# Where a preLN decoder layer's self-attention stage takes its inverse square roots: ACT's roots and DVE's reciprocals, or a power on POOL

## The chip, the cores and the metric

One core of one Trainium2 chip runs the whole kernel in one launch. The core has five engines with a queue each: PE (matrix products and transposes), DVE (vector work), ACT (scalar functions, copies with scale and bias), POOL (the general-purpose vector cores, called GpSimd) and SP (only DMA issues here). An engine works through its own instructions in program order and waits on semaphores that others raise. The metric is device time in microseconds (us), the median over runs, lower is better.

## The reference

Input `x` is 32 sequences of 128 tokens of 128 features, float32. One decoder layer is three residual blocks. Only the first (and the layer norm of the second) is touched here:

```python
def _layernorm(x, axis=-1, eps=1e-05):
    m = jnp.mean(x, axis=axis, keepdims=True)
    v = jnp.var(x, axis=axis, keepdims=True)
    return (x - m) / jnp.sqrt(v + eps)

def _L0_attn_ref(x, Wq, bq, Wk, bk, Wv, bv, Wo, bo, m):   # 16 heads of 8
    q = _l2norm(proj(Wq, bq))        # t / max(sqrt(sum t*t), 1e-12), per head
    k = _l2norm(proj(Wk, bk))
    v = proj(Wv, bv)
    sim = jnp.einsum('bhid,bhjd->bhij', q, k)
    scaling = n ** sigmoid(m)        # per head
    out = jnp.einsum('bhij,bhjd->bhid', sim / scaling, v)
    return out.transpose(0, 2, 1, 3).reshape(b, n, f) @ Wo + bo

x = x + attn(_layernorm(x))                       # stage 1, the one touched
x = x + xattn(ctx, ctx, _layernorm(x))            # exp feature maps, softmax, 77 keys
x = x + ffn(_layernorm(x))                        # top-1 of 16 experts + shared expert
```

The attention is linear (no softmax), so the kernel computes `k^T v` of each head first and multiplies by `q` afterwards.

## The kernel before

All of `x` stays in SBUF as `xs` (128 tokens on the partitions, 32 sequences, 128 features). Stage 1 (`dve_phase1`, `act_phase1`, `pool_phase1`, `pe_phase1`) works in 8 groups g of 4 sequences (`JP = 4`). It is a software pipeline written by hand: `loop1` calls an engine's `step(first, front, middle, back)` for i = -3 to 7, where `back` is group i, `middle` is i+1, `front` is i+2 and `first` is i+3, each left out where there is no such group. So i = -3, -2, -1 fill the pipeline, i = 0 to 4 are full, i = 5 lacks `first`, i = 6 lacks `front` too, and i = 7 is `back` alone. Every engine goes through the parts of a step in the order in which its own `step` is written; that order and the semaphores are all that sets who runs when.

What a group passes through:

- `first`: DVE takes mean and variance of each token (`statistics`: bn_stats L271, a small copy L163 that only waits, bn_aggr L275). ACT takes the root of variance + eps (`deviation`, L330), DVE its reciprocal and the bias -mean/std (`scale_and_bias`, L281 and L283), ACT applies both (`normalise`, L335, four instructions). POOL then adds the output bias `bo` to `xs` (L387).
- `front`: PE transposes the normalised tile (L410), ACT copies it out of PSUM (L346), PE multiplies by the q, k and v weights (L416), DVE adds the biases into `qkv` (L315).
- `middle`: ACT squares q and k (L342), DVE sums each head's squares (`ss`, L294: 4 sequences x 32 heads of q and k = 128 numbers on each of 128 partitions), ACT takes the roots (L351), DVE limits them from below (L299) and takes the reciprocals `rn` (L301), POOL multiplies q and k by them (L383, four instructions, one for each sequence). PE transposes q and forms `k^T v` (L423, L426, a pair for each sequence as POOL delivers it), DVE masks and scales it (`mt`, L320), PE multiplies by Wo (L440), ACT copies the result out (`mw`, L370).
- `back`: PE forms the output (L403), DVE adds it to `xs` (L307), and the second layer norm follows the same way as the first (`statistics`, `deviation`, `scale_and_bias`, `normalise` with k = 1). PE transposes the result (L434), and ACT copies it to `xT` (L366) for stage 2.

PE's `step` runs in the order L403, L410, L416, two products that nobody reads (`keep_streaming`, L395), the pairs L423/L426, three more of L395, L434, L440.

Ahead of stage 1 POOL has `pool_fill`: a memset of `fill` (L1343), and, once the constants have landed, a copy (L1346) and memsets of `mpart` and of two 3 x 4928 tiles `kst` (L1350). POOL enters `pool_phase1` after a wait on these. Stage 2 begins on ACT with exponentials (L543, L546).

Of the kernel before, what the change touches and what calls it, by code (L numbers as in the profile page):

```python
# [14 lines left out]
P = 128  # L15
# [14 lines left out]
def decoder_layer(nc, t, out):  # L30
# [23 lines left out]
    with ExitStack() as ctx:  # L54
# [61 lines left out]
        eps_p = sb("eps_p", [P, 1])  # L116
        carrier = sb("carrier", [P, 1])

# [11 lines left out]
        s = {}  # L130
        for n in ("const_in", "weights_in", "fill_set", "filled", "cast", "map_ready", "esc", "esc_dve",
# [3 lines left out]
                  "qres", "qmid", "qlo", "ctxTp", "ctxT", "zkp", "kf", "khi", "kres", "kmid", "klo", "vp", "v_ready",  # L135
                  "ap", "amax", "mhi", "mres", "mmid", "mlo", "mTp", "mT", "bp", "expd", "avp", "avs",
                  "ones_rows", "ones_in", "set", "tavp", "rden", "avn", "t2p", "t2", "fcp", "x2", "stat3", "mean3",
                  "xb2", "std3", "xn3", "h_kept", "hTp", "hT", "lgp", "lgT", "lgtp", "lg", "r_step", "oh", "rankp",
                  "escore", "sc_ready", "pos", "rows", "scat", "etile", "gup", "silu", "act", "downp", "x3", "tTp",
                  "tT", "tgup", "tsilu", "tact", "tyd", "ty", "res_add", "res_out"):  # L140
            s[n] = sem(n)
# [17 lines left out]

        def wait_on_copy(v, semaphore, value):  # L160

            v.wait_ge(semaphore, value)
            v.tensor_copy(carrier[:], eps[:])  # L163

# [23 lines left out]
        def dve_phase0(v):  # L188
            v.memset(eps[:], LN_EPS)
            v.memset(ones_b[:], 1.0)  # L190
            v.memset(vals[:], 1.0).then_inc(s["set"], 1)
            v.wait_ge(s["const_in"], N_CONST)
            v.tensor_copy(ident_b[:], ident[:]).then_inc(s["cast"], 1)
            v.tensor_copy(before[:], before_f[:]).then_inc(s["cast"], 1)

            v.tensor_tensor(map_w[:], map_w[:], signs[:], ALU.mult).then_inc(s["map_ready"], 1)
            v.tensor_tensor(map_b[:, 1:2], map_b[:, 0:1], signcol[:], ALU.mult).then_inc(s["map_ready"], 1)

            v.wait_ge(s["esc"], 1)
# [68 lines left out]
        def dve_phase1(v):  # L268
# [8 lines left out]

            def scale_and_bias(g, k, std_s, rstd_s, bias_s):

                v.wait_ge(s[std_s], g + 1)  # L280
                v.reciprocal(ln_rstd[k][:], ln_std[k][:]).then_inc(s[rstd_s], 1)  # L281
                v.wait_ge(s[rstd_s], g + 1)
                v.scalar_tensor_tensor(out=ln_bias[k][:], in0=ln_mv[k][:, :, 0], scalar=-1.0, in1=ln_rstd[k][:],  # L283
                                       op0=ALU.mult, op1=ALU.mult).then_inc(s[bias_s], 1)

            def step(first, front, middle, back):
                if first:
                    g, par, g2 = first
                    v.wait_ge(x_in[par], g2 * 16 + 16)
                    statistics(g, 0, "stat1", "mean1")  # L290
                if middle:
                    g, par, _ = middle
                    v.wait_ge(s["sq1"], g + 1)
                    v.tensor_reduce(ss[:], sq[:].rearrange("p j (h d) -> p (j h) d", d=HD), AX.X, ALU.add).then_inc(s["ss1"], 1)  # L294
                if first:
                    scale_and_bias(first[0], 0, "std1", "rstd1", "bias1")
                if middle:
                    v.wait_ge(s["nrm1"], g + 1)
                    v.tensor_scalar(nrm[:], nrm[:], L2_EPS, None, ALU.max).then_inc(s["nmax1"], 1)  # L299
                    v.wait_ge(s["nmax1"], g + 1)  # L300
                    v.reciprocal(rn[:], nrm[:]).then_inc(s["rn1"], 1)  # L301
                if back:
                    g, par, _ = back
                    v.wait_ge(s["yp"], g + 1)
                    v.wait_ge(s["xb1"], g + 1)
                    x_g = seqs(xs, g).rearrange("p j f -> p (j f)")
                    v.tensor_tensor(x_g, bank[7][:], x_g, ALU.add).then_inc(s["x1"], 1)  # L307
                    wait_on_copy(v, s["x1"], g + 1)
                    statistics(g, 1, "stat2", "mean2")
                    scale_and_bias(g, 1, "std2", "rstd2", "bias2")  # L310
                if front:
# [15 lines left out]
        def act_phase1(a):  # L327
            def deviation(g, k, mean, std_s):
                a.wait_ge(s[mean], g + 1)
                a.activation(ln_std[k][:], ln_mv[k][:, :, 1], ACT.Sqrt, bias=eps[:]).then_inc(s[std_s], 1)  # L330

            def normalise(g, k, bias_s, dst, done):
# [5 lines left out]
            def step(first, front, middle, back):  # L338
# [8 lines left out]
                if first:  # L347
                    deviation(first[0], 0, "mean1", "std1")
                if middle:
                    a.wait_ge(s["ss1"], middle[0] + 1)  # L350
                    a.activation(nrm[:], ss[:], ACT.Sqrt).then_inc(s["nrm1"], 1)  # L351
                if first:
                    g, par, _ = first
                    normalise(g, 0, "bias1", xn[par], "xn1")
                if back:
                    g, par, _ = back
                    deviation(g, 1, "mean2", "std2")
                    normalise(g, 1, "bias2", xn2[par], "xn2")
# [14 lines left out]

        def pool_phase1(p):
            def step(first, front, middle, back):
                if middle:

                    g, par, _ = middle
                    p.wait_ge(s["rn1"], g + 1)
                    for j in range(JP):  # L380
                        qk = qkv[par][:, j, 0:2 * D].rearrange("p (h d) -> p h d", d=HD)
                        r = rn[:, j * 2 * HEADS:(j + 1) * 2 * HEADS].rearrange("p (h o) -> p h o", o=1).broadcast_to([P, 2 * HEADS, HD])
                        p.tensor_tensor(qk, qk, r, ALU.mult).then_inc(s["qkn1"], 1)  # L383
                if first:
                    g = first[0]
# [955 lines left out]
        def pool_fill(p):  # L1341
            p.memset(eps_p[:], 0.0)
            p.memset(fill[:], 0.0).then_inc(s["fill_set"], 1)  # L1343
            p.wait_ge(s["const_in"], N_CONST)
# [100 lines left out]
```

## Time and profile before

| | |
|---|---|
| median of 3 runs | 536.94 us (532.17 to 540.25) |
| the profiled execution | 532.83 us, its span 530.8 us |
| PE busy | 420.3 us, 79% of the span |
| DVE, ACT, POOL busy | 309.2, 266.9, 219.8 us (58%, 50%, 41%) |
| mean granted TensorE clock | 0.926 of full speed |

The profile is one execution. Its page gives the busy time of each engine, the chain of work that ended last, and groups of instructions with their mean durations. The trace behind it can be asked for stretches: a timeline lists instructions by start time, with, in brackets, how long the engine had been idle before and what ended that. Times are us from the start of the span. Stage 1 runs from about 18 to 131 us, so about a fifth of the span is at stake.

### The profile page before, as it was taken

How to read it: one execution, taken by the hardware profiler on the slowest of the kernel's cores; microseconds unless marked ns; L12 is line 12 of the kernel's file. 1: busy time of each engine (PE TensorE's matmuls, PEld its weight loads, DVE VectorE, ACT ScalarE, POOL GpSimd, SP SyncE). 2: the span in 40 equal slices, each digit the busy share in tenths (PEclk: the TensorE clock that was granted, in tenths of full speed). 3: DMA queues.
4: the chain of work that ended last, by engine and by line, in shares of the span. 5: the costliest groups of instructions: out<-in, count | busy, mean ns of one | idle time of the engine just before them, and what ended most of it. 6: DMA issues, size and time to landing. Idle time of an engine off the chain costs nothing.

```text
span 530.8 us, 11018 instructions
## 1 busy us (share of the span) xinstructions
PE 420.3 (79%) x3787; PEld 308.9 (58%) x3788; DVE 309.2 (58%) x890; ACT 266.9 (50%) x610; POOL 219.8 (41%) x292
## 2 busy tenths in 40 slices
PE   0178888876877668998998999869899987999940
PEld 0146656654544436888887888623556656777730
DVE  5377878752366665777778775384753332444433
ACT  0436556444877633676776777636552212343310
POOL 4732222320577644555555000030027752666650
PEclk9999999998788767999999999969899997999985
DMA  4780000000389995676775000000023114787729
GB/s 93 176 312 1 1 0 0 2 0 0 111 227 271 281 310 137 165 194 178 192 177 151 7 5 6 1 1 1 0 76 111 52 52 109 194 267 236 229 61 297
DMA packets 52996, 62.16 MB, mean 117 GB/s; under 512 B 8366, under 2 KB 49614, under 8 KB 51278
## 3 DMA queue, kind: packets, MB, share of 16 engines
q1 hardware_dynamic: 41172, 37.86, 24.9%
q0 software_dynamic: 4864, 20.43, 13.8%
q10 hardware_dynamic: 6912, 3.25, 2.5%
q8 instruction: 28, 0.46, 0.4%
q14 instruction: 20, 0.16, 0.1%
HBM read 40.34 MB, written 20.73 MB: 115 GB/s over the span
## 4 chain that ended last, share of the span: by engine, by line
PE 50%; DVE 15%; issue 9%; ACT 9%; POOL 6%; DMA 6%; SPq 3%; ACTq 1%; DVEq 0%; POOLq 0%
PE bank L710 6%; POOL sorted_in L1192 6%; PE bank L699 5%; PE bank L1282 3%; PE bank L416 3%; PE bank L672 3%; PE bank L395 3%; PE bank L734 2%; DVE mx L777 2%; PE bank L1283 2%; PE bank L524 2%; DMA kparts<-kpart 2%; PE bank L440 2%; PE bank L1212 2%; PE bank L403 1%
## 5 line engine op out<-in xcount | busy, mean ns | idle before, releaser
L849 ACT ACTIVATE prob<-bank 77x512 f32<-77x512 f32 x128 | 74.3, 595 | 22.8 <-PE bank L699 22.6
L777 DVE TENSOR_REDUCE mx<-bank 128x5 f32<-128x385 f32 (+1 forms) x96 | 55.3, 580 | 19.4 <-PE bank L672 16.5
L1197 POOL DMA_INDIRECT routed<-t_y,t_no x48 | 46.4, 967 | 32.6 <-DVE t_y L1066 26.7
L699 PE MATMUL bank<-qst,kst 99*77 99x128 bf16 x512 | 50.2, 221 | 1.0 <-DMA qst<-mT 0.7
L1192 POOL DMA_INDIRECT sorted_in<-h_rows,pos_s x32 | 31.1, 971 | 41.6 <-issue 41.6
L383 POOL TENSOR_TENSOR qkv<-qkv,rn 128x256 f32<-128x256 f32 x32 | 19.1, 627 | 63.7 <-DVE rn L301 63.7
L699 PEld LDWEIGHTS bank<-qst,kst 99*77 99x77 bf16 x512 | 38.4, 116 | 8.7 <-ACT prob L849 4.3
L672 PE MATMUL bank<-kst,qst 96*128 96x77 bf16 x512 | 35.4, 205 | 6.2 <-DVE mx L777 4.0
L1059 DVE TENSOR_TENSOR t_act<-bank,t_sg 128x128 f32<-128x128 f32 x48 | 14.0, 291 | 41.8 <-ACT t_sg L1151 41.8
L1147 ACT COPY t_hT<-bank 128x128 f32<-128x128 f32 x48 | 12.7, 265 | 49.6 <-PE bank L1273 43.8
L637 POOL DMA_DIRECT2D qst<-qparts x36 | 18.2, 505 | 46.4 <-DMA kst<-kparts 31.8
L960 DVE TENSOR_TENSOR act<-bank,s_g 128x512 f32<-128x512 f32 x24 | 16.5, 688 | 31.5 <-ACT s_g L1134 31.4
L1223 PEld LDWEIGHTS bank<-sd,act 128*128 128x128 f32 x192 | 25.3, 194 | 15.4 <-issue 9.6
L710 PE MATMUL bank<-prob,vals 77*17 77x128 f32 x1024 | 34.2, 274 | 0.0
L1134 ACT ACTIVATE s_g<-bank 128x512 f32<-128x512 f32 x24 | 14.2, 597 | 38.2 <-PE bank L1234 38.2
L335 ACT ACTIVATE xn<-xs,ln_bias,ln_rstd 128x128 f32<-128x128 f32 (+1 forms) x64 | 26.4, 482 | 11.4 <-DVE ln_bias L283 11.4
L571 DVE TENSOR_TENSOR res_q<-qkv,qpart 128x512 f32<-128x512 f32 x16 | 14.6, 911 | 30.0 <-ACT qpart L546 30.0
L672 PEld LDWEIGHTS bank<-kst,qst 96*128 96x128 bf16 x512 | 26.8, 101 | 8.0 <-DVE mx L777 6.0
L416 PE MATMUL bank<-wqkv,xnT 128*128 128x384 f32 x64 | 24.7, 532 | 6.8 <-ACT xnT L346 6.8
L395 PE MATMUL bank<-wqkv,ident_s 128*128 128x384 f32 x80 | 29.2, 497 | 0.0
L1223 PE MATMUL bank<-sd,act 128*128 128x128 f32 x192 | 26.2, 280 | 3.1 <-DVE act L960 3.1
L1282 PEld LDWEIGHTS bank<-t_hT,t_w 128*128 128x128 f32 x96 | 16.2, 196 | 18.3 <-ACT t_hT L1147 13.8
(178 smaller groups left out, 1068.0 us busy)
## 6 DMA issues: line engine op xcount, KB each, us to landing
qst<-qparts POOLq DMA_DIRECT2D x36, 256.0 KB, 3.5
t_w<-in_expert_w SPq DMA_DIRECT2D x48, 192.0 KB
qparts<-qpart SPq DMA_DIRECT2D x16, 384.0 KB, 7.4
kst<-kparts POOLq DMA_DIRECT2D x36, 154.0 KB, 3.8
kparts<-kpart SPq DMA_DIRECT2D x16, 231.0 KB, 7.7
sorted_in<-fill SPq DMA_DIRECT2D x1, 3168.0 KB, 10.3
t_row<-sorted_in ACTq DMA_DIRECT2D x48, 66.0 KB
qst<-qparts SPq DMA_DIRECT2D x12, 256.0 KB, 6.5
```

What stands on the lines that cost most here:

```text
L335: i = a.activation(dst[:, j], x_of(g, j), ACT.Identity, scale=ln_rstd[k][:, j:j + 1], bias=ln_bias[k][:, j:j + 1])
L395: pe.matmul(bank[0][:, 0:3 * D], ident[:], wqkv[:], start=True, stop=True)
L416: pe.matmul(bank[1 + j][:, 0:3 * D], xnT[par][:, j * P:(j + 1) * P], wqkv[:], start=True, stop=True).then_inc(s["qkvp"], 1)
L672: i = pe.matmul(bank[n % 2][:, (h - h0) * KEYS:(h - h0 + 1) * KEYS], qst[r][0:ROWS, h, c * S:(c + 1) * S], kst[r][0:ROWS, h, c * KEYS:(c + ...
L699: i = pe.matmul(bank[2 + n % 2][0:KEYS, c * S:(c + 1) * S], kst[r][0:SHIFT_ROWS, h, t * KEYS:(t + 1) * KEYS], qst[r][0:SHIFT_ROWS, h, t * ...
L710: i = pe.matmul(bank[AV_BANK[b % 2]][32 * c:32 * c + EX + 1, u * P:(u + 1) * P], vals[:, b, 4 * u + c], prob[n % PROBS][:, c], start=True, ...
L777: v.tensor_reduce(mx[:, b % JA, h0:h1], bank[n % 2][:, 0:(h1 - h0) * KEYS].rearrange("p (h k) -> p h k", k=KEYS), AX.X, ALU.max, negate=Tr ...
L849: a.activation(prob[n % PROBS][:].rearrange("p c t -> p (c t)"), bank[2 + n % 2][0:KEYS], ACT.Exp, scale=SCORE_SCALE).then_inc(s["expd"], 1)
L1192: p.indirect_dma_start(out=sorted_in, out_offset=bass.IndirectOffsetOnAxis(ap=pos[:, b:b + 1].bitcast(U32), axis=0), in_=h_rows[:, b], in_ ...
L1197: p.indirect_dma_start(out=routed, out_offset=bass.IndirectOffsetOnAxis(ap=t_no[r][:].bitcast(U32), axis=0), in_=t_y[r][:], in_offset=None ...
L1223: i = pe.matmul(bank[BK_DOWN[par]][:, j * D:(j + 1) * D], act[c][:, j * P:(j + 1) * P], sd[:, c], start=(c == 0 and j == 0), stop=(c == CH ...
L1282: pe.matmul(bank[2 + r % 2][:, 0:P], t_w[r][:, 0:FF], t_hT[r % 2][:], start=True, stop=True)
```

## The change

In stage 1 every inverse root is now a power of -0.5 on POOL. ACT's `deviation` and its root of the squares go, and so do DVE's `scale_and_bias` and reciprocals. For a layer norm POOL does four instructions, each waiting for the one before: variance + eps, the power, mean times the result, and zero minus that. For q and k DVE limits the sums of squares from below (by the square of the old limit), and POOL takes the power of the 128 x 128 tile. POOL's `step` is ordered `first`'s scale and bias, the power for `middle`, its four products, `back`'s scale and bias, the bias add of `first`. Since single buffers hold the norms' values, DVE waits for `bias1` before the next group's statistics, for `bias2` before L307's new place (L302), and for `rn1` before it overwrites `nrm`.

```diff
@@ DVE
-            def scale_and_bias(g, k, std_s, rstd_s, bias_s):
-                v.wait_ge(s[std_s], g + 1)
-                v.reciprocal(ln_rstd[k][:], ln_std[k][:]).then_inc(s[rstd_s], 1)
-                v.wait_ge(s[rstd_s], g + 1)
-                v.scalar_tensor_tensor(out=ln_bias[k][:], in0=ln_mv[k][:, :, 0], scalar=-1.0, in1=ln_rstd[k][:],
-                                       op0=ALU.mult, op1=ALU.mult).then_inc(s[bias_s], 1)
                 if first:
                     g, par, g2 = first
+                    if not is_first(g):
+                        wait_on_copy(v, s["bias1"], g, 1)
                     v.wait_ge(x_in[par], g2 * 16 + 16)
                     statistics(g, 0, "stat1", "mean1")
                 if middle:
-                if first:
-                    scale_and_bias(first[0], 0, "std1", "rstd1", "bias1")
-                if middle:
-                    v.wait_ge(s["nrm1"], g + 1)
-                    v.tensor_scalar(nrm[:], nrm[:], L2_EPS, None, ALU.max).then_inc(s["nmax1"], 1)
-                    v.wait_ge(s["nmax1"], g + 1)
-                    v.reciprocal(rn[:], nrm[:]).then_inc(s["rn1"], 1)
+                    v.wait_ge(s["ss1"], g + 1)
+                    if not is_first(g):
+                        v.wait_ge(s["rn1"], g)
+                    v.tensor_scalar(nrm[:], ss[:], L2_EPS * L2_EPS, None, ALU.max).then_inc(s["nmax1"], 1)
                 if back:
                     v.wait_ge(s["yp"], g + 1)
                     v.wait_ge(s["xb1"], g + 1)
+                    if not is_first(g):
+                        v.wait_ge(s["bias2"], g)
-                    scale_and_bias(g, 1, "std2", "rstd2", "bias2")
@@ ACT
-            def deviation(g, k, mean, std_s):
-                a.wait_ge(s[mean], g + 1)
-                a.activation(ln_std[k][:], ln_mv[k][:, :, 1], ACT.Sqrt, bias=eps[:]).then_inc(s[std_s], 1)
-                if first:
-                    deviation(first[0], 0, "mean1", "std1")
-                if middle:
-                    a.wait_ge(s["ss1"], middle[0] + 1)
-                    a.activation(nrm[:], ss[:], ACT.Sqrt).then_inc(s["nrm1"], 1)
                 if back:
-                    deviation(g, 1, "mean2", "std2")
@@ POOL
+            def scale_and_bias(g, k, mean, std_s, rstd_s, bias_s):
+                p.wait_ge(s[mean], g + 1)
+                if k == 1 and not is_first(g):
+                    p.wait_ge(s["xn2"], g)
+                p.tensor_tensor(ln_std[k][:], ln_mv[k][:, :, 1], eps[:].broadcast_to([P, JP]), ALU.add).then_inc(s[std_s], 1)
+                p.wait_ge(s[std_s], g + 1)
+                p.tensor_tensor(ln_rstd[k][:], ln_std[k][:], power[:].broadcast_to([P, JP]), ALU.pow).then_inc(s[rstd_s], 1)
+                p.wait_ge(s[rstd_s], g + 1)
+                p.tensor_tensor(ln_mean[k][:], ln_mv[k][:, :, 0], ln_rstd[k][:], ALU.mult).then_inc(s[std_s + "m"], 1)
+                p.wait_ge(s[std_s + "m"], g + 1)
+                p.tensor_tensor(ln_bias[k][:], eps_p[:].broadcast_to([P, JP]), ln_mean[k][:], ALU.subtract).then_inc(s[bias_s], 1)
             def step(first, front, middle, back):
+                if first:
+                    scale_and_bias(first[0], 0, "mean1", "std1", "rstd1", "bias1")
                 if middle:
+                    p.wait_ge(s["nmax1"], g + 1)
+                    p.tensor_tensor(rn[:], nrm[:], power[:].broadcast_to([P, JP * 2 * HEADS]), ALU.pow).then_inc(s["rn1"], 1)
                     p.wait_ge(s["rn1"], g + 1)
                     ...
+                if back:
+                    scale_and_bias(back[0], 1, "mean2", "std2", "rstd2", "bias2")
@@ pool_fill
             p.memset(eps_p[:], 0.0)
+            p.memset(power[:], -0.5)
```

Where the instructions stand. POOL, from the end of `pool_fill` into stage 1, before (`kst` are the tiles of the two memsets):

```order
L1350 MEMSET kst_90 3x4928 [waits ones_rows]
L1350 MEMSET kst_91 3x4928 [waits ones_rows]
L387 ISA
L387 TENSOR_TENSOR xs<-xs,bo 128x512 [waits xn1,const_in,ones_rows]
L387 TENSOR_TENSOR xs<-xs,bo 128x512 [waits xn1]
L383 TENSOR_TENSOR qkv<-qkv,rn 128x256 [waits rn1]
```

And of the change:

```order
L1354 MEMSET kst_92 3x4928 [waits ones_rows]
L1354 MEMSET kst_93 3x4928 [waits ones_rows]
L364 ISA
L364 TENSOR_TENSOR ln_std_53<-ln_mv_51,eps 128x4 [waits mean1,const_in,ones_rows]
L366 TENSOR_TENSOR ln_rstd_55<-ln_std_53,power 128x4 [waits std1]
L368 TENSOR_TENSOR ln_mean_57<-ln_mv_51,ln_rstd_55 128x4 [waits rstd1]
L370 TENSOR_TENSOR ln_bias_59<-eps_p,ln_mean_57 128x4 [waits std1m]
L390 TENSOR_TENSOR xs<-xs,bo 128x512 [waits xn1]
L364 TENSOR_TENSOR ln_std_53<-ln_mv_51,eps 128x4 [waits mean1]
```

The first norm's scale and bias now stand behind the memsets on POOL; what stood there before was the bias add, which comes after the norm.

POOL in a full step, before:

```order
L383 TENSOR_TENSOR qkv<-qkv,rn 128x256 [waits rn1]
L383 TENSOR_TENSOR qkv<-qkv,rn 128x256 x3
L386 REGISTER_ALU
L387 ISA [waits xn1]
L387 TENSOR_TENSOR xs<-xs,bo 128x512
```

And of the change, from the power of the q and k norms on (the four instructions of `first` stand ahead of it):

```order
L379 TENSOR_TENSOR rn<-nrm,power 128x128 [waits nmax1]
L384 TENSOR_TENSOR qkv<-qkv,rn 128x256 [waits rn1]
L384 TENSOR_TENSOR qkv<-qkv,rn 128x256 x3
L361 REGISTER_ALU
L364 TENSOR_TENSOR ln_std_54<-ln_mv_52,eps 128x4 [waits xn2,mean2]
L366 TENSOR_TENSOR ln_rstd_56<-ln_std_54,power 128x4 [waits std2]
L368 TENSOR_TENSOR ln_mean_58<-ln_mv_52,ln_rstd_56 128x4 [waits rstd2]
L370 TENSOR_TENSOR ln_bias_60<-eps_p,ln_mean_58 128x4 [waits std2m]
L390 ISA [waits xn1]
L390 TENSOR_TENSOR xs<-xs,bo 128x512
```

The power now comes ahead of the four products on the same engine, and the second norm's scale and bias come behind them.

DVE in a full step, from the sum of squares to the add into `xs`, before:

```order
L294 TENSOR_REDUCE ss<-sq 128x128 [waits sq1]
L281 RECIPROCAL ln_rstd_55<-ln_std_53 128x4 [waits std1]
L283 SCALAR_TENSOR_TENSOR ln_bias_57<-ln_mv_51,ln_rstd_55 128x4 [waits rstd1]
L299 TENSOR_SCALAR nrm<-nrm 128x128 [waits nrm1]
L301 RECIPROCAL rn<-nrm 128x128 [waits nmax1]
L304 REGISTER_ALU
L307 ISA [waits xb1,yp]
L307 TENSOR_TENSOR xs<-bank,xs 128x512
```

And of the change:

```order
L290 TENSOR_REDUCE ss<-sq 128x128 [waits sq1]
L293 REGISTER_ALU [waits ss1]
L294 TENSOR_SCALAR nrm<-ss 128x128 [waits rn1]
L302 ISA [waits bias2,xb1,yp]
L302 TENSOR_TENSOR xs<-bank,xs 128x512
```

Both reciprocals and the bias product are gone, and so is the wait for ACT's root between the sum and the limit.

## Rows read from the trace of the kernel before

**Rows 1.** Windows: stretch, length, PE, PEld, DVE, ACT, POOL busy, clock, DMA.
```profile
52.33:64.46 12.13, 10.56 (x54) 7.40 (x55) 9.63 (x32) 7.17 (x17) 3.62 (x5) 1.00 0.00 1
112.00:124.50 12.50, 9.11 (x42) 6.71 (x43) 5.41 (x17) 5.32 (x11) 2.38 (x4) 0.86 0.00 0
```

**Rows 2.** Timeline, full step i = 1: start, duration, engine, line, [idle before].
```profile
52.33 1.13 PE L403 MATMUL bank<-mw,qT 128*128 128x128 f32 x8 [0.77 <-ACT mw L370]
53.18 1.22 DVE L294 TENSOR_REDUCE ss<-sq 128x128 f32<-128x1024 f32 x1 [1.57 <-ACT sq L342]
54.66 2.84 PE L416 MATMUL bank<-wqkv,xnT 128*128 128x384 f32 x8 [0.76 <-ACT xnT L346]
...
56.33 2.39 POOL L383 TENSOR_TENSOR qkv<-qkv,rn 128x256 f32<-128x256 f32 x4 [8.51 <-DVE rn L301]
...
59.62 0.27 PE L423 MATMUL bank<-ident_s,qkv 128*128 128x128 f32 x1
...
60.10 1.65 ACT L335 ACTIVATE xn<-xs,ln_bias,ln_rstd 128x128 f32 x4 [1.53 <-DVE ln_bias L283]
61.75 0.73 DVE L320 SCALAR_TENSOR_TENSOR mt<-bank,inv_scale,headmask_s 128x512 f32<-128x512 f32 x1
61.89 0.60 PE L434 MATMUL bank<-ident_s,xn 128*128 128x128 f32 x4
```

**Rows 3.** Timeline of the start of stage 1.
```profile
17.15 8.46 POOL L1350 MEMSET kst<- 3x4928 bf16 x2
19.39 1.28 ACT L330 ACT_TABLE_LOAD   x1 [1.46 <-DVE ln_mv L275]
21.22 0.16 DVE L283 SCALAR_TENSOR_TENSOR ln_bias<-ln_mv,ln_rstd 128x4 f32<-128x4 f32 x1
```

**Rows 4.** Timeline of step i = -1, its `middle`.
```profile
34.38 2.39 POOL L383 TENSOR_TENSOR qkv<-qkv,rn 128x256 f32<-128x256 f32 x4 [5.83 <-DVE rn L301]
...
36.94 0.27 PE L423 MATMUL bank<-ident_s,qkv 128*128 128x128 f32 x1
```

**Rows 5.** Timeline of steps i = 6 and i = 7.
```profile
113.45 1.22 DVE L294 TENSOR_REDUCE ss<-sq 128x128 f32<-128x1024 f32 x1 [3.69 <-ACT sq L342]
116.34 2.38 POOL L383 TENSOR_TENSOR qkv<-qkv,rn 128x256 f32<-128x256 f32 x4 [9.35 <-DVE rn L301]
...
127.44 0.37 DVE L275 BATCH_NORM_AGGREGATE ln_mv<-ln_stats 128x2 f32<-128x6 f32 x4
128.59 1.65 ACT L335 ACTIVATE xn<-xs,ln_bias,ln_rstd 128x128 f32<-128x128 f32 x4 [0.44 <-DVE ln_bias L283]
```

**Rows 6.** Timeline of the start of stage 2 on ACT.
```profile
132.92 1.28 ACT L543 ACT_TABLE_LOAD   x1
...
134.39 0.52 ACT L543 ACTIVATE kf<-bank,map_b 128x308 f32<-128x308 f32 x1 [0.18 <-PE bank L520]
```

**Rows 7.** Groups by line on POOL: busy us, mean ns, idle before.
```profile
L1192 POOL DMA_INDIRECT sorted_in<-h_rows,pos_s x32 | 31.1, 971 | 41.6 <-issue 41.6
L383 POOL TENSOR_TENSOR qkv<-qkv,rn 128x256 f32<-128x256 f32 x32 | 19.1, 627 | 63.7 <-DVE rn L301 63.7
...
L387 POOL TENSOR_TENSOR xs<-xs,bo 128x512 f32 x4 | 5.1, 1269 | 0.0
...
L1184 POOL COPY h_rows<-token_no 128x32 int32<-128x32 int32 x1 | 0.2, 238 | 0.1
...
L1342 POOL MEMSET eps_p<- 128x1 f32 x1 | 0.1, 99 | 0.3 <-POOLq L1435 0.3
```

**Rows 8.** Groups by line on DVE, 0 to 125 us.
```profile
L301 DVE RECIPROCAL rn<-nrm 128x128 f32<-128x128 f32 x8 | 7.6, 953 | 0.3
L283 DVE SCALAR_TENSOR_TENSOR ln_bias<-ln_mv,ln_rstd 128x4 f32<-128x4 f32 x15 | 7.4, 494 | 0.5
...
L307 DVE TENSOR_TENSOR xs<-bank,xs 128x512 f32 x4 | 2.5, 628 | 0.0
...
L299 DVE TENSOR_SCALAR nrm<-nrm 128x128 f32<-128x128 f32 x8 | 1.8, 222 | 0.8 <-ACT nrm L351 0.8
```

More of the change, by code:

```diff
@@ L116, in decoder_layer @@
         eps_p = sb("eps_p", [P, 1])
-        carrier = sb("carrier", [P, 1])
+        power = sb("power", [P, 1])
+        carrier = sb("carrier", [P, 2])
         xs = sb("xs", [P, B, D])
@@ L130, in decoder_layer @@
         s = {}
-        for n in ("const_in", "weights_in", "fill_set", "filled", "cast", "map_ready", "esc", "esc_dve",
+        for n in ("const_in", "weights_in", "fill_set", "filled", "std2m", "map_ready", "esc", "esc_dve",
                   "inv_ready", "stat1", "mean1", "std1", "rstd1", "bias1", "xn1", "xT1p", "xT1", "qkvp", "qkv1",
[1 row of a table removed]
[1 row of a table added]
                   "xb1", "x1", "stat2", "mean2", "std2", "rstd2", "bias2", "xn2", "xT2p", "xT2", "zqp", "qf", "qhi",
@@ L136, in decoder_layer @@
                   "ap", "amax", "mhi", "mres", "mmid", "mlo", "mTp", "mT", "bp", "expd", "avp", "avs",
-                  "ones_rows", "ones_in", "set", "tavp", "rden", "avn", "t2p", "t2", "fcp", "x2", "stat3", "mean3",
+                  "ones_rows", "ones_in", "std1m", "set", "tavp", "rden", "avn", "t2p", "t2", "fcp", "x2", "stat3", "mean3",
                   "xb2", "std3", "xn3", "h_kept", "hTp", "hT", "lgp", "lgT", "lgtp", "lg", "r_step", "oh", "rankp",
@@ L158, in is_first, with wait_on_copy @@
             return isinstance(g, int) and g == 0
-        def wait_on_copy(v, semaphore, value):
+        def wait_on_copy(v, semaphore, value, k=0):
             v.wait_ge(semaphore, value)
-            v.tensor_copy(carrier[:], eps[:])
+            v.tensor_copy(carrier[:, k:k + 1], eps[:])
         CONSTS = [(ident, "ident"), (headmask, "headmask"), (signs, "signs"), (signcol, "signcol"),
@@ L192, in dve_phase0 @@
             v.wait_ge(s["const_in"], N_CONST)
-            v.tensor_copy(ident_b[:], ident[:]).then_inc(s["cast"], 1)
-            v.tensor_copy(before[:], before_f[:]).then_inc(s["cast"], 1)
+            v.tensor_copy(ident_b[:], ident[:])
+            v.tensor_copy(before[:], before_f[:])
             v.tensor_tensor(map_w[:], map_w[:], signs[:], ALU.mult).then_inc(s["map_ready"], 1)
@@ L225, in decoder_layer @@
         ln_rstd = [sb1(f"ln_rstd{k}", [P, JP]) for k in range(2)]
+        ln_mean = [sb1(f"ln_mean{k}", [P, JP]) for k in range(2)]
         ln_bias = [sb1(f"ln_bias{k}", [P, JP]) for k in range(2)]
```

>
> **The small ones, S.** Each norm now needs four dependent instructions of 128 x 4. POOL's smallest rows are 99 ns (memset, one element) and 238 ns (copy, 32 elements) [rows 7]. I take 0.15 for each of three, and 0.15 + 4 x 31 ns = 0.28 for the power; with 0.05 for each of four handoffs inside the engine (assumed) S = 0.93, say 0.95, between 0.6 and 1.5.
>
> **The start.** POOL's two memsets of `kst` run from 17.15 to 25.61 [rows 3]. Before, the first norm didn't need POOL: its bias was ready at 21.38 (21.22 + 0.16), a table load of 1.28 for ACT's root included. Now its four instructions stand behind the memsets: 25.61 + 0.08 + 0.95 = 26.64. Everything behind, PE's first matmul included, starts **5.3** later. Group 1's norm then waits for POOL's bias add of group 0, but PE needs it only after the slow first L416, so this is hidden.
>
> *Rule and row.* Removing ACT's roots also removes two table loads. In the trace each takes 1.28: the first stands in the start's chain, and the second, at stage 2's first exponential, is followed by a further 0.18 of waiting for PE [rows 6], so it is hidden and worth 0. The Trainium skill ("ScalarE: Activation LUTs", What ACT_TABLE_LOAD costs) speaks of about 2.7 us a load, and by its figure two loads would be worth some 5 us, an estimate that would cancel the late start. The measured duration decides, and the start above already counts the first load's 1.28 as saved.
>
> **Step i = -1.** Between the end of the sum and POOL's first product there were 1.67 us (114.67 to 116.34 in [rows 5]; the other steps have the same parts). Now there are 0.03 + 0.22 (limit) + 0.08 + P + 0.05 = 0.38 + P. POOL is later by P - 1.29. The products ended at 36.77, PE's last L423 began at 36.94 [rows 4], with a handoff a slack of about 0.12: cost P - 1.4 = **2.6**.
>
> **Steps i = 0 to 5.** From L403's start (52.33): the sum ends at 2.07, limit and handoffs bring the power's start to 2.40. Then P, 0.05, products 2.39, S for the second norm, 0.05, ACT's 1.65, 0.09: L434 can start at 6.63 + P + S. It started at 9.56. The delay is P + S - 2.93 = **2.02 a step**. The products alone would delay the last L423 by less (P - 2.4 = 1.6), and it is absorbed in the same wait. Nothing else in the step hides it: the next L403 follows from L440 and an ACT copy. Six such steps: **12.1**. `first`'s norm has most of a step of time on POOL and costs nothing; POOL's load, 3.62 + P + 2S = 9.5, is below the step's length.
>
> **Steps i = 6 and 7.** In i = 6 there is no `front`, and PE waited for POOL before too: P - 1.29 = **2.7**. In i = 7 the last norm is bare: from DVE's 127.81 to ACT's 128.59 there were 0.78 [rows 5], now 0.08 + 0.95 + 0.08, **0.3** more.
>
> **Sum.** 5.3 + 2.6 + 12.1 + 2.7 + 0.3 = 23.0. Against the profiled execution's 532.83 that is 555.8. This execution is near the lower end of the three runs; on their median of 536.94 it is 560, which I predict. As a formula: 8P - 9.0 + the clock's loss, if any, with S = 0.95.
>
> *The rule against the change.* POOL takes 1269 ns for a two-input pass of 128 x 512 and DVE 628 for one [rows 7, 8]: twice. The Trainium skill ("GPSIMD Engine Reference", 4.1 Engine selection) gives the same factor and sends elementwise work to VectorE. By that rule alone the power would be a plain pass (P = 0.3, an estimate) and the change would cost the late start only, which is the cheap rival below.
>
> **Rivals.**
> - *The power is cheap* (P below 2.4): the full steps stay at 12.13. The cost is the start, 5.3, plus or minus little: with P = 0.31 and S = 0.6 it is 4.9 - 1.0 (i = 6) = +3.9, or 541; at P = 2.4, +10.5. For it speaks that POOL is 16 lanes in 8 cores and the plain pass is a loop with room in it; against it, that a power is not one operation. Chance 0.27.
> - *The power is dear and PE's clock falls* (P above 6.5). In i = 6 PE idled 2 us and the window's clock was 0.86 [rows 1]; full steps had 1.00. If waits of 4 us and more a step do this, each step's PE work stretches too, by about 0.14 x 12 = 1.7 to 2. With P = 6.5: 43 + 11 = 54, or 591; with P = 10 over 620. Chance 0.18.
> - *Faster.* DVE, not PE, binds the full steps: `mt` ends 0.01 from L434's end [rows 2], and since PE's ends are modelled, DVE could be what leads. Then the removed reciprocal (0.95) and two bias products (0.49 each) [rows 8] would shorten six steps by up to 11.6, which less the late start of 5.3 is a gain of 6.3: 531. It needs P + S below 2.9 and PE able to run its order in 10.2, where it is busy for 10.56 and waits 1.5 on its own copies; only if a third of PE's busy time were slack would it pass 2%. Chance 0.03.
> - *Forecast* (P from 2.4 to 6.5): 0.52.
>
> **Numbers.** The range reaches from 539 (cheap, with the low profiled base) to 592 (where the dear case begins). A measurement of this kernel can tell about 2% (10.7 us) from no change; the sum passes it at P = 2.46, so the cheap case is "same". Faster 0.03, same 0.27, slower 0.70.
>
> **What would show it.** In the changed profile: the first normalisation starts at about 26.7, behind POOL's memsets (wrong if earlier). The power's row on 128 x 128 reads 4.0 us and the four small ones 0.15 to 0.3. PE waits for POOL's products and for ACT's L434 input in each full step, step length 14.15 at clock 1.00. Table loads are two fewer, without effect in stage 2. Stages 2 to 4 keep their lengths. The prediction is wrong in size, not in kind, if P is elsewhere; it is wrong in kind if full steps get shorter than 12.13.

## The result and the profile after

The changed kernel takes 702.75 us (696.93 to 705.12, 4 runs) against 534.56 us (531.57 to 540.25, 4 runs) of the kernel before: 1.315 times the time, 95% interval 1.308 to 1.322. The direction was forecast; the size, 560 with 592 as the upper end, was far too small.

The groups of instructions by line of the changed kernel name the cause at once (busy us, mean ns, then idle before):

```profile
L379 POOL TENSOR_TENSOR rn<-nrm,power 128x128 f32<-128x128 f32 x8 | 165.8, 20727 | 28.7 <-DVE nrm L294 28.7
...
L384 POOL TENSOR_TENSOR qkv<-qkv,rn 128x256 f32<-128x256 f32 x32 | 19.1, 628 | 0.6
...
L366 POOL TENSOR_TENSOR ln_rstd<-ln_std,power 128x4 f32<-128x4 f32 x16 | 16.3, 1017 | 1.3
```

The power of the 128 x 128 tile takes 20.73 us, where I had put P = 4.0. The small power takes 1.02 where I had 0.28. The wide one is the same to 0.02 us in all 8 calls, the small one to 0.04 in its 16.

One full step (i = 1) of the changed kernel as a timeline, which answers to [rows 2]:

```profile
98.92 1.13 PE L406 MATMUL bank<-mw,qT 128*128 128x128 f32 x8 [0.77 <-ACT mw L354]
99.77 1.22 DVE L290 TENSOR_REDUCE ss<-sq 128x128 f32<-128x1024 f32 x1 [3.57 <-ACT sq L332]
...
101.32 20.73 POOL L379 TENSOR_TENSOR rn<-nrm,power 128x128 f32<-128x128 f32 x1 [3.20 <-DVE nrm L294]
...
122.13 2.39 POOL L384 TENSOR_TENSOR qkv<-qkv,rn 128x256 f32<-128x256 f32 x4
122.81 0.47 PE L426 MATMUL bank<-ident_s,qkv 128*128 128x128 f32 x1 [17.44 <-POOL qkv L384]
...
124.47 0.20 POOL L364 TENSOR_TENSOR ln_std<-ln_mv,eps 128x4 f32<-128x4 f32 x1
124.75 1.01 POOL L366 TENSOR_TENSOR ln_rstd<-ln_std,power 128x4 f32<-128x4 f32 x1
...
126.12 0.20 POOL L370 TENSOR_TENSOR ln_bias<-eps_p,ln_mean 128x4 f32<-128x4 f32 x1
...
126.77 1.65 ACT L325 ACTIVATE xn<-xs,ln_bias,ln_rstd 128x128 f32 x4 [24.11 <-POOL ln_bias L370]
...
128.47 0.66 PE L437 MATMUL bank<-ident_s,xn 128*128 128x128 f32 x4 [0.51 <-ACT xn L325]
...
130.79 0.46 PE L406 MATMUL bank<-mw,qT 128*128 128x128 f32 x2 [0.77 <-ACT mw L354]
```

The chain is the one that the prediction wrote down: the sum, the limit, the power at 2.40 after the step's start (101.32 - 98.92), the products, the second norm behind them on POOL, ACT, then PE. PE stands still for 17.44 us ahead of its first pair. The windows of this step and of a later one give the clock (length, PE, PEld, DVE, ACT, POOL busy, granted clock, DMA):

```profile
98.92:130.79 31.87, 12.40 (x54) 8.75 (x55) 7.43 (x28) 6.38 (x14) 27.52 (x14) 0.73 0.00 0
163.10:194.74 31.64, 12.68 (x54) 8.92 (x55) 7.38 (x28) 6.37 (x14) 27.51 (x14) 0.73 0.00 0
```

The mean granted clock is 0.73 where it was 1.00 [rows 1]. POOL is busy for 27.5 of 31.9 us.

Stage 2 begins (PE's first product of that stage) at 298.82 instead of 131.62, 167.2 us later. What follows took 404.3 us in this profile and 399.2 in that of before. The prediction said that these stages keep their lengths; both profiles are single executions, the runs of either kernel spread over 8 to 9 us, and these 5 us aren't located.

The start of stage 1, answering to [rows 3]:

```profile
17.09 8.46 POOL L1354 MEMSET kst<- 3x4928 bf16 x2
...
25.64 0.20 POOL L364 TENSOR_TENSOR ln_std<-ln_mv,eps 128x4 f32<-128x4 f32 x1
25.92 1.04 POOL L366 TENSOR_TENSOR ln_rstd<-ln_std,power 128x4 f32<-128x4 f32 x1
27.04 0.20 POOL L368 TENSOR_TENSOR ln_mean<-ln_mv,ln_rstd 128x4 f32<-128x4 f32 x1
27.32 0.20 POOL L370 TENSOR_TENSOR ln_bias<-eps_p,ln_mean 128x4 f32<-128x4 f32 x1
...
27.63 1.65 ACT L325 ACTIVATE xn<-xs,ln_bias,ln_rstd 128x128 f32<-128x128 f32 x4 [9.76 <-POOL ln_bias L370]
```

The norm's four instructions start as the memsets end, as forecast; they take 1.88 together (25.64 to 27.52), three of 0.20, one of 1.04 and gaps of 0.08.

### The profile page after: what moved, and what is told of

Read it like the earlier page. It is cut to its first block, busy times and chain, and to the rows that moved or that the text cites. A ratio compares the mean times of both kernels' runs of the same rounds, so it can differ in the third digit from the quotient of the medians.

```text
span 703.1 us, 11049 instructions
## 1 busy us (share of the span) xinstructions
PE 439.0 (62%) x3787; PEld 324.1 (46%) x3788; DVE 295.8 (42%) x857; ACT 258.3 (37%) x584; POOL 411.5 (59%) x365
## 3 DMA queue, kind: packets, MB, share of 16 engines
HBM read 40.34 MB, written 20.73 MB: 87 GB/s over the span
## 4 chain that ended last, share of the span: by engine, by line
PE 34%; POOL 32%; DVE 8%; DMA 7%; issue 7%; ACT 7%; SPq 3%; ACTq 1%; DVEq 0%; POOLq 0%
POOL rn L379 24%; POOL sorted_in L1195 4%; PE bank L713 4%; PE bank L702 3%; DMA qparts<-qpart 3%; PE bank L1285 2%; DMA kst<-kparts 2%; PE bank L398 2%; PE bank L675 2%; PE bank L737 2%; PE bank L1286 2%; PE bank L429 1%; DVE ss L290 1%; POOL qkv L384 1%; PE bank L1215 1%
## 5 line engine op out<-in xcount | busy, mean ns | idle before, releaser
L379 POOL TENSOR_TENSOR rn<-nrm,power 128x128 f32<-128x128 f32 x8 | 165.8, 20727 | 28.7 <-DVE nrm L294 28.7
L426 PE MATMUL bank<-ident_s,qkv 128*128 128x128 f32 x32 | 13.9, 435 | 142.0 <-POOL qkv L384 142.0
L314 DVE SCALAR_TENSOR_TENSOR mt<-bank,inv_scale,headmask_s 128x512 f32<-128x512 f32 x8 | 6.0, 750 | 165.1 <-PE bank L429 165.1
L426 PEld LDWEIGHTS bank<-ident_s,qkv 128*128 128x128 f32 x32 | 6.2, 195 | 146.9 <-POOL qkv L384 146.9
L398 PE MATMUL bank<-wqkv,ident_s 128*128 128x384 f32 x80 | 34.8, 575 | 0.0
L1226 PEld LDWEIGHTS bank<-sd,act 128*128 128x128 f32 x192 | 24.9, 192 | 15.5 <-issue 9.7
L419 PE MATMUL bank<-wqkv,xnT 128*128 128x384 f32 x64 | 26.3, 561 | 6.8 <-ACT xnT L336 6.8
```

Source lines behind the costliest of these rows:

```text
L379: p.tensor_tensor(rn[:], nrm[:], power[:].broadcast_to([P, JP * 2 * HEADS]), ALU.pow).then_inc(s["rn1"], 1)
L398: pe.matmul(bank[0][:, 0:3 * D], ident[:], wqkv[:], start=True, stop=True)
L419: pe.matmul(bank[1 + j][:, 0:3 * D], xnT[par][:, j * P:(j + 1) * P], wqkv[:], start=True, stop=True).then_inc(s["qkvp"], 1)
L1226: i = pe.matmul(bank[BK_DOWN[par]][:, j * D:(j + 1) * D], act[c][:, j * P:(j + 1) * P], sd[:, c], start=(c == 0 and j == 0), stop=(c == CH ...
```

## The experiments

Two theories stand against each other. *Price*: the step law of the prediction is right, and only P and S were mis-sized. *Placement*: the order on POOL, the new waits of DVE for POOL, and the handoffs cost by themselves. Ratios are to the kernel before on the same chip. x2, x3, x4 and x7 keep the order of the instructions but compute something else: their q and k, or half of them, are zero, and in x3 and x4 the norms are wrong too. They are for timing alone.

**x1: what a power costs.** Twelve instructions ahead of stage 1 on POOL, in tiles not yet in use:

```diff
+            one(P, 4, 0, 0, ALU.pow)      # partitions, width, tile (0: 1.0, 1: 37.3), exponent (0: -0.5 ... 3: 2.0)
+            one(P, 32, 0, 0, ALU.pow)
+            ...
+            one(P, 128, 1, 3, ALU.pow)
+            one(1, 128, 1, 0, ALU.pow)
+            one(P, 4, 1, 0, ALU.mult)
```

> The kernel before, with twelve POOL instructions added ahead of stage 1, each waiting for the one before; only their durations matter. Powers with exponent -0.5 of a tile of ones, 4, 32, 64 and 128 wide on 128 partitions; 128 wide on a tile of 37.3 with exponents -0.5, 0.5, -1.0 and 2.0; the same with -0.5 on a single partition; then a product of 4 and of 128 and a subtraction of 128. Theory 'fixed price for an element column': 0.38 us + 0.159 us a column, whatever the value and exponent: 1.0, 5.5, 10.6, 20.7 us for the four widths and 20.7 for the rest, the product 0.3. Whether the cores work on 16 partitions at once or one after another is told by the single partition: 20.7 if at once, about 1.7 if one after another. Rival 'the value decides': ones, or the exponents 2.0 and -1.0, cost a fraction of 20.7.

The groups of these instructions by shape (one line of the kernel; 128 x 128 holds five powers, a product and a subtraction, 128 x 4 a power and a product):

```profile
L1355 POOL TENSOR_TENSOR fill<-fill 128x128 f32<-128x128 f32 x7 | 104.4, 14912 | 0.5
L1355 POOL TENSOR_TENSOR fill<-fill 1x128 f32<-1x128 f32 x1 | 20.7, 20705 | 0.1
L1355 POOL TENSOR_TENSOR fill<-fill 128x64 f32<-128x64 f32 x1 | 10.5, 10519 | 0.1
...
L1355 POOL TENSOR_TENSOR fill<-fill 128x32 f32<-128x32 f32 x1 | 5.4, 5418 | 0.1
...
L1355 POOL TENSOR_TENSOR fill<-fill 128x4 f32<-128x4 f32 x2 | 1.3, 628 | 0.2
```

From 32 to 64 columns the power grows by 5.10 us, from 64 to 128 by 10.2: 159 ns a column and 0.32 fixed. A single partition costs 20.7 as well, where it would have been about 1.7 if partitions were taken one after another. No power of 128 columns took more than 20.73, and five of them together some 103.6 (104.4 less about 0.8 for the two plain passes), so ones and 37.3, and the exponents -0.5, 0.5, -1 and 2, cost the same. So do the kernel's own values (20.72 to 20.74 in the changed kernel). The price goes by the column, and by none of the partitions, values and exponents tried. It is 65 times the plain product's 2.45 ns a column [rows 7].

**x2 and x3: the same placement with a cheap operation.**

```diff
-p.tensor_tensor(rn[:], nrm[:], power[:].broadcast_to(...), ALU.pow)
+p.tensor_tensor(rn[:], nrm[:], eps_p[:].broadcast_to(...), ALU.mult)     # x2 and x3
-p.tensor_tensor(ln_rstd[k][:], ln_std[k][:], power[:]..., ALU.pow)
+p.tensor_tensor(ln_rstd[k][:], ln_std[k][:], power[:]..., ALU.mult)      # x3 too, power = 1.0
```

> The changed kernel with the q and k norm's power replaced by a product with zero on the same tile, at the same place (so q and k come out zero); all else as changed. Theory 'price': the step law holds with P = 0.31 and the measured S = 1.88: start +6.1, full steps +0 (12.13 us), i = 6 -1.0, i = 7 +1.3, in all +6.4 us on the kernel before, about 541 and a ratio of 1.012. Rival 'placement': the waits across POOL's queue and DVE's new waits for POOL cost by themselves, full steps stay several us longer than 12.13 and the kernel stays above 560.

> The changed kernel with both kinds of power replaced by products (q and k come out zero, the norms scale by the variance). Theory 'price': S = 1.05, start +5.3, full steps +0, i = 6 -1.0, i = 7 +0.4: +4.7 us on the kernel before, ratio 1.009, and 1.7 us below the kernel with the norms' powers left in. Rival 'placement': as much above the kernel before as that one, or more than 10 us.

x2: 537.39 us, ratio 1.0085 (1.004 to 1.013). x3: 534.03 us, ratio 0.9965 (0.993 to 1.000). Placement falls: of the 168 us, 165 go when one operation is exchanged in its place (702.75 to 537.39). But both came out below what I expected, by 4 and 6 us. The traces locate 0.7 and 2.2 us of this in stage 1 (stage 2 begins 5.7 and 2.5 later than before, against 6.4 and 4.7 expected); the rest isn't located. The part in stage 1 can be seen in a step of x3, from 69.27 to 81.08:

```profile
76.88 2.10 PE L398 MATMUL bank<-wqkv,ident_s 128*128 128x384 f32 x6
77.08 0.75 DVE L314 SCALAR_TENSOR_TENSOR mt<-bank,inv_scale,headmask_s 128x512 f32<-128x512 f32 x1 [1.41 <-PE bank L429]
...
78.82 0.60 PE L437 MATMUL bank<-ident_s,xn 128*128 128x128 f32 x4
...
79.26 1.06 PE L443 MATMUL bank<-wo,mt 128*128 128x128 f32 x8
```

A full step takes 11.81 us, not 12.13. `mt` is what PE loads as weights for L443 (L440 before). Here it is ready at 77.83, 1.3 us ahead of that load, which lies under the matmuls ahead. In the kernel before the load waited for DVE; its weight loads (PEld) read

```profile
62.53 0.97 PEld L440 LDWEIGHTS bank<-wo,mt 128*128 128x128 f32 x8 [0.28 <-DVE mt L320]
```

and in x3

```profile
67.33 0.97 PEld L443 LDWEIGHTS bank<-wo,mt 128*128 128x128 f32 x8
```

with no wait. That is the 0.3 us a step. The slack of 0.01 between `mt` and L434's end was no slack. That x3 works on zeros isn't the reason, since x8, with q and k as they should be, has the same step (11.82). Step i = 6 fell to 10.31 from 11.91, more than the 1.0 that I expected; its mean clock was 1.00 here and 0.86 before.

The prediction overlooked why `mt` was so late. It read DVE's two bias products of a step as 0.49 each [rows 8], but that is a mean of two kinds. In the step of [rows 2] the second of them stands beside POOL's bias add:

```profile
58.68 1.26 POOL L387 TENSOR_TENSOR xs<-xs,bo 128x512 f32 x1
...
58.81 1.15 DVE L283 SCALAR_TENSOR_TENSOR ln_bias<-ln_mv,ln_rstd 128x4 f32<-128x4 f32 x1
```

It takes 1.15 instead of 0.16, ends 0.02 behind POOL's add, and does so in each full step of the kernel before; in steps i = 5 and 6, where POOL has no such add, it takes 0.16, `mt` isn't awaited, and step i = 5 took 11.74. So DVE was held by POOL for about 1.0 us a step, and moving this product to POOL took it out of DVE's way. POOL's power holds nothing of the kind: in x6 the same product runs beside it in 0.16.

**x4: where the late start comes from.** As x3, with the memsets of `mpart` and `kst` ahead of POOL's wait for the constants.

```diff
             p.memset(fill[:], 0.0).then_inc(s["fill_set"], 1)
+            p.memset(mpart[:], 0.0) ...; the two memsets of kst; p.wait_ge(s["ones_rows"], 3)
             p.wait_ge(s["const_in"], N_CONST)
```

> As the kernel with both powers replaced by products, and POOL's memsets of mpart and kst moved ahead of its wait for the constants, where it idles. Theory 'late start is POOL's queue': the first norm's bias is ready at about 20.4 instead of 26.7, the kernel 6.3 us below the one without the move and 1 to 2 us below the kernel before (ratio 0.997). Rival: the start is bound by something else (x, the constants, DVE's wait for the bias), and the move gives under 2 us.

526.83 us, ratio 0.984 (0.976 to 0.993), and in the traces the first L406 starts at 39.01 instead of 45.63: 6.6 us, as expected of POOL's queue. The late start is a matter of order on POOL alone. The kernel lies 8 us below the one before, where I had expected 1 to 2. Most of this miss is that of x3, which already lay 5.6 below its expectation.

**x5 and x6: each half of the change alone.**

```diff
 x5: the norms as changed; q and k as before:
-p.wait_ge(s["nmax1"], g + 1); p.tensor_tensor(rn, nrm, power, ALU.pow)
+a.activation(nrm, ss, ACT.Sqrt); v.tensor_scalar(..., ALU.max); v.reciprocal(rn, nrm)
 x6: the norms as before (ACT.Sqrt, v.reciprocal, bias on DVE); q and k as changed
```

> Half of the change: the layer norms' inverse roots as a power on POOL (S = 1.88), the q and k norm by ACT's root and DVE's reciprocal as before. Theory 'price by the step law': the first bias 6.1 later; in full steps POOL is through with the products at 6.4 after L403 and with the norm at 8.3, so the second norm's input comes some 0.5 late, less 0.3 that the earlier mask product on DVE gives back: steps of about 12.35; last norm +1.3. Together +8 to +9 us on the kernel before, ratio 1.016. Rival 'any power on POOL in the step is ruinous': over +30 us.

> The other half: the q and k norm as a power on POOL (20.73 us), the layer norms on ACT and DVE as before. Theory 'price by the step law': no late start; step i = -1 +19.3; each of six full steps P - 2.44 = 18.3 longer; i = 6 +19.4: +148 us, about 683, ratio 1.28, some 20 us below the whole change. Rival 'the norms' four instructions are the main loss, the wide power overlaps with other work': under +80 us.

x5: 540.66 us, ratio 1.0105 (1.004 to 1.017), 5 us more than before where I had expected 8 to 9; in its trace stage 2 begins 8.6 later, and its full steps take 12.08, not 12.35. x6: 693.77 us, ratio 1.297 (1.290 to 1.303), 158 us more than before. So the wide power is nearly all of it. x6 lies 10 us above its expectation, and its steps i = 0 to 5 take 32.3 in the mean, more than the whole change's 31.9, though the norm isn't behind the products. Its window of a step, and PE at the end of that step:

```profile
94.59:127.58 32.99, 13.42 (x54) 9.38 (x55) 7.99 (x31) 7.13 (x16) 24.34 (x6) 0.69 0.00 1
```

```profile
121.28 0.63 PE L426 MATMUL bank<-qkv 128*128 128x128 f32 x2
121.70 3.78 PE L395 MATMUL bank<-wqkv,ident_s 128*128 128x384 f32 x6
125.32 0.60 PE L434 MATMUL bank<-ident_s,xn 128*128 128x128 f32 x4
```

The three filler products take 3.78 us here, and took 2.10 in x3's step at clock 1.00: after its wait of 18 us PE runs at the lower of its two clock levels, 1.2 GHz (granted clock 0.50 from 119.1 to 124.9), until about L434. In x6 this stretch is on the path: the steps are 1.9 longer than by the law (32.3 against 30.4), and the filler alone takes 1.7 more. In the whole change it is mostly hidden, because PE would wait for the second norm anyway (L437 waits 0.51 for ACT in the step shown above), and there the law holds nearly without a term for the clock: the six steps are 118.9 longer, by the law 118.1.

**x7: half the width.**

```diff
-p.tensor_tensor(rn[:], nrm[:], power..., ALU.pow)
+p.tensor_tensor(rn[:, 64:128], nrm[:, 64:128], eps_p..., ALU.mult)
+p.tensor_tensor(rn[:, 0:64], nrm[:, 0:64], power..., ALU.pow)
```

> The changed kernel with the power on the first 64 of the 128 columns and a product with zero on the others (so half of q and k come out zero). One size changed: P = 10.52 + 0.28 instead of 20.73. Theory 'the loss is 8 times P': 8 x 9.9 = 79 us less than the changed kernel, about 624. Rival 'a threshold, or the clock': a loss that doesn't go with the width, more than 15 us away from that.

622.07 us (a single run): 81 below the changed kernel, against 79 by the law; in the traces stage 2's first exponential starts 78.4 earlier. The loss goes with the width, eight times over.

**x8: the inverse roots where they are cheap.** If DVE's reciprocals cost 0.3 a step and something at the ends, ACT can give the inverse root in one instruction. This kernel leaves out the limit from below, so a head of zeros isn't guarded.

```diff
-a.activation(ln_std, var, ACT.Sqrt, bias=eps);  v.reciprocal(ln_rstd, ln_std)
+a.activation(ln_rstd, var, ACT.Abs_reciprocal_sqrt, bias=eps)
-a.activation(nrm, ss, ACT.Sqrt);  v.tensor_scalar(nrm, ..., ALU.max);  v.reciprocal(rn, nrm)
+a.activation(rn, ss, ACT.Abs_reciprocal_sqrt)
+a.activation(early_root, m_col, ACT.Abs_reciprocal_sqrt)     # once, ahead of stage 1
```

> The kernel before with both inverse roots taken by ACT in one instruction (its absolute reciprocal root), so without DVE's reciprocals and limit, POOL as before; and an idle use of that function ahead of stage 1, so that its table load lies in ACT's wait. Theory 'what the roots cost before was 0.3 a step by the late mask product, and the chains at the ends': steps 11.81, i = 6 1.2 to 1.5 less, start 1.3 to 1.5 less, i = 7 0.2 less: 5 us less than before, ratio 0.990. Rival 'PE's order is the bound alone': full steps stay 12.13 and the gain is under 3 us.

525.32 us, ratio 0.981 (0.976 to 0.985). In the trace the full steps behind the first take 11.82 at clock 1.00, and i = 6 takes 9.51 instead of 11.91; stage 2 begins at 126.70 instead of 131.62, 4.9 us earlier. I had expected 5, but that the sum came out is partly luck: the start gives 1.9, the six steps 0.4 instead of some 1.6, i = 6 gives 2.4 instead of 1.2 to 1.5. The windows of its first two full steps show where the steps fell short:

```profile
38.31:51.36 13.05, 11.53 (x55) 8.49 (x55) 8.27 (x28) 7.17 (x17) 3.61 (x5) 0.87 0.00 1
51.36:63.18 11.82, 10.30 (x55) 7.42 (x55) 8.37 (x28) 7.17 (x17) 3.62 (x5) 1.00 0.00 1
```

The first step is 1.2 longer at a mean clock of 0.87; why the clock fell there stays open. The medians differ by 10 us, twice what stage 1 gives. The rest isn't located: the profiles are single executions, stages 2 to 4 took 399.2 us in the profile of before and 399.7 in x8's, and the runs of either kernel spread over 8 to 11 us.

**x9 and x10: what binds once DVE is relieved.** Both leave out PE's filler.

```diff
 def keep_streaming(n):
-    for _ in range(n): pe.matmul(bank[0][:, 0:3 * D], ident[:], wqkv[:], start=True, stop=True)
+    pass
```

> The kernel before without PE's products that nobody reads (five a full step, 3.23 us). Theory 'mt and POOL stand right beside PE': with the filler gone DVE's order sets the step (its mask product ends 10.15 after L403, whatever PE does): steps of 11.9 to 12.1, at most 2 us gained, or a loss if PE's granted clock falls with its idle time. Rival 'PE's order alone is the bound': steps of about 9, over 15 us gained.

> The inverse roots on ACT with the early table load, and without PE's filler products. Theory: the relieved DVE ends its mask product about 8.0 after L403, steps of about 10.1 at full clock, some 10 us below the same kernel with the filler; if the clock falls in these steps (below 1.00), most or all of it is lost. Rival: steps stay 11.8, since ACT or POOL bind them.

x9, the kernel before without filler: 540.19 us, ratio 1.014 (1.004 to 1.023), slower. Its steps i = 0 to 3 take 13.0 to 13.5. x10, the roots on ACT and no filler: **519.74 us, ratio 0.976 (0.960 to 0.992)**, faster than the kernel before. Its median is 5.6 below x8's, where I had expected 10; the intervals of the two overlap, but in the traces stage 2 begins 7.2 earlier. The windows, first of x9, then of x10:

```profile
52.00:64.00 12.00, 8.43 (x43) 6.49 (x44) 9.64 (x32) 6.72 (x16) 3.62 (x5) 0.91 0.01 2
...
76.00:88.00 12.00, 10.48 (x40) 7.65 (x39) 7.26 (x27) 5.17 (x13) 3.61 (x5) 0.60 0.00 0
```

```profile
58.00:68.00 10.00, 6.81 (x40) 4.88 (x39) 7.50 (x25) 6.58 (x15) 3.62 (x5) 1.00 0.00 0
68.00:78.00 10.00, 6.89 (x40) 5.21 (x40) 7.58 (x28) 6.64 (x16) 3.62 (x5) 1.00 0.00 0
```

In x9 DVE's chain sets the step. In most steps PE waits some 2.4 us for ACT's normalisation, which waited for DVE's bias product, again held to 1.15 by POOL's add. Its clock falls (0.60 in one window): the eight products with `mt` take 1.94 and 2.07 in two of these steps, and 1.16 with filler. That makes the step longer than with filler. In x10 the first step takes 12.16 at a clock of 0.72; in the next four the shorter chain keeps the step at 10.80 and the clock at 1.00. There too PE waits for ACT's normalisation, 1.64 us, behind a bias product on DVE that POOL's add holds to 1.09:

```profile
64.19 1.27 POOL L385 TENSOR_TENSOR xs<-xs,bo 128x512 f32 x1
...
64.39 1.09 DVE L284 SCALAR_TENSOR_TENSOR ln_bias<-ln_mv,ln_rstd 128x4 f32<-128x4 f32 x1 [0.36 <-ACT ln_rstd L328]
...
67.32 0.65 PE L431 MATMUL bank<-ident_s,xn 128*128 128x128 f32 x4 [1.64 <-ACT xn L333]
...
68.06 0.97 PEld L437 LDWEIGHTS bank<-wo,mt 128*128 128x128 f32 x8 [0.32 <-DVE mt L318]
```

The last line shows `mt` awaited again. DVE works from the held product to `mt` without a pause, so both of PE's waits hang on it. No run moves POOL's add; it is the next thing to try.

## Why the prediction was wrong

- **The price P was mis-sized by five; this is the step that failed.** The prediction priced the power from DVE's reciprocal (4.3 plain passes), as two such functions and a product, 3.0, and then took 4.0. Measured: 20.73. Even its upper bound, 15.5 from the indirect DMA's cost per row, was below that. The ratio of a function to a plain pass was carried from DVE to POOL, with no row for it; on POOL it is 159 ns a column, 65 plain passes (x1), not 9.6. Why a power costs POOL this much, no run shows. The 0.18 chance of the "dear" rival, which ran "over 620", was the case that came.
- **The range was cut where the bound was not.** I had written P = 15.5 as the far end and then set the range's top at P = 6.5. By the recorded formula, 8P - 9.0, P = 15.5 gives +115, 652 us; a range that kept the far end would still have missed, by 51 instead of 111. The lower end, 539, doesn't follow from its own terms either: 532.83 + 3.9 is 536.7.
- **The small price S was mis-sized by two**: 1.88 against 0.95. The small power is 1.02, each plain one 0.20 and each gap 0.08.
- **The step law held.** With the measured P and S, L437 can start at 6.63 + 20.73 + 1.88 = 29.24 after the step's start; it did at 29.55. The handoff from POOL to ACT took 0.45 where 0.05 was assumed; the other terms gave 0.09 back. Term by term, from the traces of before and after: start +6.2 (law 6.2), i = -1 +20.9 (19.3; there the power stood 0.5 behind the first norm in POOL's queue, and PE then ran at a clock of 0.50), the six steps +118.9 (118.1), i = 6 +19.6 (19.4), i = 7 +1.6 (1.3). Together stage 2 starts 167.2 us later; the law gives 164.3, and the medians differ by 168.2. x7 confirms the slope, x2 and x3 that nothing but the price is behind it.
- **The late start was right**: POOL's queue (x4: 6.6 us back by order alone). The first normalisation starts at 27.63, where 26.7 was forecast, the 0.9 being the error in S. The second table load was worth nothing, as forecast: ACT's first exponential of stage 2 starts 1.49 after the copy ahead of it without the load (x3, the first two rows) and with it (x5):

```profile
135.03 0.41 ACT L553 COPY ctxT_s<-bank 128x308 f32<-128x308 f32 x1 [0.92 <-PE bank L517]
136.93 0.52 ACT L546 ACTIVATE kf<-bank,map_b 128x308 f32<-128x308 f32 x1 [1.48 <-PE bank L523]
```

```profile
141.12 0.41 ACT L554 COPY ctxT_s<-bank 128x308 f32<-128x308 f32 x1 [0.92 <-PE bank L518]
141.56 1.28 ACT L547 ACT_TABLE_LOAD   x1
143.02 0.52 ACT L547 ACTIVATE kf<-bank,map_b 128x308 f32<-128x308 f32 x1 [0.18 <-PE bank L524]
```

The prediction set the measured 1.28 against some 2.7 in the Trainium skill ("ScalarE: Activation LUTs", What ACT_TABLE_LOAD costs). That section gives 1283 ns for the load itself, which is what every load takes here, and a drain for the rest of its total. The two don't differ on the load, and no row here shows the drain: in x5 the load starts 0.03 behind the copy.

- **"What DVE and ACT are relieved of can't shorten a full step" was wrong, by 0.3 a step.** `mt` is a weight operand, and its load waited for DVE. The rival "faster" had named the right place, though neither the weight load nor that POOL's add held DVE (x2 and x3 above), and x3, x8 and x10 show what it is worth: 12.13 to 11.81 a step with the filler, 10.80 without.
- **The clock** fell as the dear rival said (0.73), but cost under 1 us in the change's steps i = 0 to 5 together, since PE waited for the second norm meanwhile; where that wait is gone (x6), the steps are 1.9 longer than the law.

## What to carry to other kernels

A function has no price on an engine until a row of that engine shows one: bound it by what is known, keep the far bound in the range, or measure it alone first, as x1 does. Look at the spread behind a mean: 0.49 was 0.16 and 1.15. When two engines end together, look at the weight loads too: an operand that arrives "just in time" for a matmul is late for its load. Relieve the second-tightest engine first and take out clock-keeping filler afterwards; in the other order (x9) it costs.

## What the runs showed of the hardware

- POOL's power of float32: 0.32 us + 159 ns for each column, the same on 1 partition as on 128, for 1.0 as for 37.3, and for the four exponents tried. A plain product, also on this engine: 0.20 for 4 columns, 2.45 ns a column for wide tiles.
- ACT's absolute reciprocal root of 128 x 128 takes 0.30 us, 69 times less than POOL's power. The group in x8 (busy us, mean ns, idle before):

```profile
L349 ACT ACTIVATE rn<-ss 128x128 f32<-128x128 f32 x8 | 2.4, 302 | 1.9 <-DVE ss L295 1.9
```

- DVE's bias product of 128x4 takes 0.16 us alone and 1.15 when it starts during POOL's add of 128x512, ending 0.02 behind it (before, each full step). During POOL's power it takes 0.16 (x6).
- PE's mean granted clock was 0.73 in steps with a wait of 17 us, 0.66 to 0.94 in x9's steps i = 0 to 5, four of which have a wait of some 2.4 us, and 1.00 in x10's steps i = 1 to 4, where the longest wait is 1.6 us, though PE is busy for about the same share or less. No run varies the length of this wait alone, and the first steps of x8 and x10, at 0.87 and 0.72, don't have it longer; what sets the clock here stays open.
